# A gated cross-attention block on one core: exponent scores two steps behind the maximum scores, another owner of a bank's release, and GpSimd's rounding last in its step

## The reference, cut to what matters

```python
x = x + tanh(g_xattn[0]) * attention(layernorm(x), ctx, ctx)        # 16 heads, no projections, no mask
x = x + tanh(g_ffn[0])   * fp8_gemm(layernorm(x))                   # rounded to float8_e4m3, 256 x 256
x = x + tanh(g_xattn[1]) * masked_attention(layernorm(x), ctx)      # with projections q, k, v, o
x = x + tanh(g_ffn[1])   * ternary_ffn(layernorm(x))                # fake-quantised over the whole tensor
```

## Time and profile before

| | us |
|---|---|
| median of 3 runs | 3008.16 (3006.38 to 3012.38) |
| the profiled execution | 3008.19 |
| its span, first to last instruction | 3006.2 |

### The profile page before, as it was taken

How to read it: one execution, slowest core, us unless ns; L and a number is a source line. 1 busy time by engine, 2 the same in 40 slices (tenths; PEclk the granted TensorE clock), 3 DMA queues, 4 the chain that set the end, 5 groups by cost and what they waited for, 6 DMA issues and landing times. The chain is left out here.

```text
span 3006.2 us, 82393 instructions
## 1 busy us (share of the span) xinstructions
PE 2519.7 (84%) x28184; PEld 1800.6 (60%) x28184; DVE 2110.6 (70%) x6142; ACT 1789.5 (60%) x3015; POOL 1487.8 (49%) x2143
## 2 busy tenths in 40 slices
PE   3767777777777765999999999999999999999566
PEld 2445455555545544777777777777777777777344
DVE  4666666666666665778777877787778778878344
ACT  2666666666666663666566666665666666656355
POOL 2555555555555553444444544444444444444377
PEclk9998989899899997999999999999999999999756
DMA  2101111011110100000000000000000000000023
GB/s 68 33 29 31 31 31 31 28 31 31 31 31 28 32 14 17 18 19 18 19 19 16 21 17 18 19 18 19 19 19 18 16 19 19 18 19 13 22 101 102
DMA packets 99578, 82.87 MB, mean 28 GB/s; under 512 B 14928, under 2 KB 99280, under 8 KB 99280
## 3 DMA queue, kind: packets, MB, share of 16 engines
q1 hardware_dynamic: 99280, 78.88, 8.7%
HBM read 61.02 MB, written 16.78 MB: 26 GB/s over the span
## 5 line engine op out<-in xcount | busy, mean ns | idle before, releaser
L906 DVE TENSOR_REDUCE nmax<-bank_max 128x8 f32<-128x1024 f32 x256 | 312.6, 1221 | 371.5 <-DVEq L905 371.5
L617 ACT ACTIVATE stk<-bank_t 128x1024 bf16<-128x1024 bf16 x384 | 390.7, 1017 | 122.4 <-PE bank_t L1189 122.0
L649 ACT ACTIVATE stk<-bank_exp 128x1024 f32<-128x1024 f32 x256 | 262.0, 1023 | 201.7 <-ACTq L648 197.7
L622 ACT ACTIVATE probs<-bank_exp 128x512 f32<-128x512 f32 x512 | 288.8, 589 | 156.7 <-PE bank_exp L1169 156.7
L875 DVE TENSOR_REDUCE nmax<-bank_max 128x4 f32<-128x512 f32 x512 | 349.4, 683 | 31.9 <-PE bank_max L1156 31.7
L1218 PE MATMUL bank_max<-parts,QK 32*128 32x256 f32 x2048 | 333.2, 448 | 1.5 <-PEq L1281 1.5
L1225 PE MATMUL bank_exp<-parts,QK 32*128 32x256 f32 x2048 | 307.8, 421 | 0.0
L1189 PE MATMUL bank_t<-ident,parts 128*128 128x128 bf16 x4096 | 294.0, 220 | 2.6 <-PEq L1340 2.1
L487 POOL TENSOR_TENSOR rstd_f<-stat_f,eps_col 128x1 f32<-128x1 f32 x128 | 24.4, 191 | 522.5 <-POOLq L561 522.5
L1189 PEld LDWEIGHTS bank_t<-ident,parts 128*128 128x128 bf16 x4096 | 252.5, 98 | 21.6 <-issue 3.0
L1351 PE MATMUL bank_m<-wT,QK 128*128 128x256 f32 x1024 | 252.7, 391 | 1.2 <-PEq L1347 1.2
(11 more groups left out here) (181 smaller groups left out, 6647.5 us busy)
## 6 DMA issues: line engine op xcount, KB each, us to landing
X<-in_x SPq DMA_DIRECT2D x128, 128.0 KB, 2.1
stk<-in_ctx SPq DMA_DIRECT2D x128, 128.0 KB, 2.1
QK<-in_ctx SPq DMA_DIRECT2D x128, 128.0 KB, 2.1
out_y<-X SPq DMA_DIRECT2D x64, 256.0 KB, 2.1
ff_qq<-in_mask_BxSxS_ik SPq DMA_DIRECT2D x128, 64.0 KB, 1.9
stk<-shift_T SPq DMA_DIRECT2D x128, 8.0 KB
X<-in_L_xattn_Wq SPq DMA_DIRECT2D x1, 256.0 KB, 6.9
X<-in_L_xattn_Wk SPq DMA_DIRECT2D x1, 256.0 KB, 7.2
```

Source lines behind the costliest of these rows:

```text
L617: nc.scalar.activation(stk[k2][:, :, g * HG:(g + 1) * HG, :].rearrange("p w h t -> p w (h t)"), bank_tb[bank].rearrange("p (w n) -> p w n" ...
L622: nc.scalar.activation(probs[g % 2][:, :, :], bank_exp[g % 2][:, :, :], ACT.Exp, scale=SCALE).then_inc(probs_made, 1)
L649: nc.scalar.activation(a_probs[n], exp_pair[:, :, :, :].rearrange("p i h t -> p (i h) t"), ACT.Exp, scale=SCALE).then_inc(probs_made, 1)
L906: return v.tensor_reduce(nmax[:, n * H // 2:(n + 1) * H // 2], max_pair[:, :, :, :].rearrange("p i h t -> p (i h) t"), axis=AX.X, op=ALU.m ...
```

## The change

Six things change in pass A:

- Exponent scores are computed for batch i − 2 instead of i − 1; the shift transposes and their copy now have a step of their own in between. What follows them moves too: weighing at −2, the division at −3, the feed-forward part by 1 to 4 steps more.
- TensorE's step begins with `fill(0)`; then the transposes of weighed sums, the input transposes, the shift transposes, the feed-forward product (even steps), `fill(1)`, weighing 1, the transposes of rounded inputs (odd steps), weighing 0. Before `fill(0)` it waits for the second `max_read` of the previous step.
- VectorE signals `attn_read` itself when `attn_normed` has ended (before, GpSimd did when it took the residual); `attn_x` to GpSimd now comes with the following `bn_aggr`.
- GpSimd's step: statistics first (odd), masks, residual, V, and the rounding last (even steps); before, the rounding came first (odd) and the statistics last.
- ScalarE's step: exponential 1, copy of inputs, copy of shifts, copy of y (even), norms (feed-forward in odd steps, both attention inputs in even steps), exponential 0, copy of rounded inputs (odd), copy of weighed sums.
- Tiles: `sh_T`, `a_y` and the maxima (`a_nmax`) get two copies. New semaphores `stats_read`, `y_used`, `fq_used`. `hand_back` no longer drains. x is fetched one step earlier. 19 and 21 steps are unrolled at the ends instead of 12 and 15.

The diff, cut to its core:

```diff
-        sh_T = probs_b[1][:, 0:4 * P]
+        sh_T = [probs_b[1][:, n * 4 * P:(n + 1) * 4 * P] for n in range(2)]
...
-        A_LO, A_HI, A_FIRST, A_LAST = -6, NB + 5, 6, 6 + (NB - 12) // UNROLL * UNROLL
+        A_LO, A_HI, A_FIRST, A_LAST = -7, NB + 9, 12, 12 + (NB - 20) // UNROLL * UNROLL
...
             def hand_back():
-                mine(pool.drain())
+                if not own[0]:
+                    return
                 pool.wait_ge(pool_own, own[0])
...
+                if odd and (live(3) or live(-5)):
+                    s = k // 2 % 2
+                    pool.wait_ge(stats_made, 1)
...
+                    settle()
+                    pool.sem_inc(stats_read, 1)
...
+                if live(-3):
+                    pool.wait_ge(attn_x, 1)
+                    pool.sem_inc(attn_x, -1)
+                    nc.gpsimd.tensor_tensor(xs(i - 3), xs(i - 3), attn[:, :], ALU.add).then_inc(x_added, 1)
...
+                if not odd and live(-6):
+                    pool.wait_ge(grid_made, 1)
+                    pool.sem_inc(grid_made, -1)
+                    mine(nc.gpsimd.tensor_tensor(a_t, a_t, a_e, ALU.add))
                     settle()
+                    if live(-8):
+                        pool.wait_ge(fq_used, 1)
+                        pool.sem_inc(fq_used, -1)
+                    nc.gpsimd.tensor_tensor(ff_qq[:, :, :].rearrange("p b n -> p (b n)"), a_t, a_e, ALU.subtract)\
+                      .then_inc(fq_made, 1)
...
+                if live(-2):
+                    exp_pair_of(1)
                 if live(1):
                     act.wait_ge(in_Td, 1)
...
+                    nc.scalar.activation(sh_T[(k + 1) % 2], bank_tb[1][:, 0:4 * P], ACT.Copy).then_inc(shift_out, 1)
...
+                if not odd and live(2):
+                    for n in range(2):
+                        normed(a_xn[n], i + 2 + n, (k // 2 + 1) % 2, 2 + n).then_inc(xn_made, 1)
+                if live(-2):
+                    exp_pair_of(0)
...
+                if live(-3):
                     settle(n_rden)
-                    attn_normed().then_inc(attn_x, 1)
+                    attn_normed().then_inc(attn_read, 1)
+                if odd and (live(5) or live(-3)) and (live(1) or live(-7)):
+                    vec.wait_ge(stats_read, 1)
+                    vec.sem_inc(stats_read, -1)
...
+                if live(0):
+                    n_max = mine(max_pair_of(1, k % 2))
+                    settle(n_max)
+                    vec.sem_inc(max_read, 1)
+                    n_hi = mine(v.tensor_copy(sh_v[:, :, :, 0], a_nmax[:, k % 2, :].rearrange("p (i b) -> p i b", i=4)))
...
+                if not odd and live(-10):
+                    settle(n_y)
+                    v.scalar_tensor_tensor(xs2(i - 10), y.rearrange("p b n -> p (b n)"), gate[:, 2:3],
+                                           xs2(i - 10), ALU.mult, ALU.add).then_inc(y_used, 1)
...
-                now, last4 = k % RING, (k + 3) % RING
+                now = k % RING if live(0) else None
+                before = (k + 2) % RING if live(-2) else None
                 if live(0):
                     pe.wait_ge(m_made, 1)
                     pe.sem_inc(m_made, -1)
                 if live(-1):
-                    pe.wait_ge(shift_made, 1)
-                    pe.sem_inc(shift_made, -1)
...
+                    pe.wait_ge(max_read, 1)
+                    pe.sem_inc(max_read, -1)
+                fill(0, now, before, k % 2)
+                if live(-3):
+                    attn_transpose()
```

More of the change, by code:

```diff
@@ L243, in build @@
         norm_made = sem("norm_made")
+        stats_read = sem("stats_read")
+        y_used = sem("y_used")
+        fq_used = sem("fq_used")
         fx_made = sem("fx_made")
@@ L958, in step_a @@
                     settle()
                     vec.sem_inc(stats_made, 1)
-                if not odd and live(-4):
+                if odd and live(-5):
                     vec.wait_ge(fx_made, 1)
@@ L1206, in attn_transpose, with fill @@
                 last.then_inc(attn_back, 1)
[L1208 removed]
+            def fill(n, now, before, ring):
                 lo, hi = 2 * n, 2 * (1 - n)
@@ L1265, in step_a @@
                     last.then_inc(in_Td, 1)
+                if not odd and live(-8):
+                    pe.wait_ge(fq_out, 1)
+                    pe.sem_inc(fq_out, -1)
+                if live(-1):
+                    pe.wait_ge(shift_made, 1)
+                    pe.sem_inc(shift_made, -1)
+                    for b in range(4):
+                        last = nc.tensor.transpose(bank_tb[1][:, b * P:(b + 1) * P], sh[:, b * P:(b + 1) * P],
+                                                   ident[:, :])
+                    last.then_inc(shift_Td, 1)
+                if not odd and live(-8):
+                    for b in range(2):
+                        for c in range(DC):
+                            last = mm(bank_m[:, b * D:(b + 1) * D], ff_qT2[:, DC * b + c, :], f8_w[:, c, :],
+                                      start=c == 0, stop=c == DC - 1)
+                    last.then_inc(fy_made, 1)
+                if live(0):
+                    pe.wait_ge(max_read, 1)
+                    pe.sem_inc(max_read, -1)
+                if live(-2):
+                    pe.wait_ge(probs_made, 1)
+                fill(1, now, before, k % 2)
                 if live(-1):
```

183 lines of the change are left out of this document (73 added, 110 removed).

## The result

The changed kernel takes 2823.23 us (2821.82 to 2825.69, four runs) against 3008.68 us (3006.38 to 3012.38) for the kernel before on the same chip: a ratio of 0.938, with a 95% interval of 0.937 to 0.940. The forecast was 2808, with a range of 2745 to 2885. The profiled span went from 3006.2 to 2820.6 us.

The account below looks back on a forecast made before the run. No engine was full; a closed chain through four engines took turns for 8.0 us. 64 pairs going from 16.96 to 13.75 us save 205.4 us, the ends cost 5: 3008.2 − 200.4 = 2807.8 us, range 2745 to 2885.

Parts of the forecast that it names:

- the closed chain of the even step: Transposes, copy, scores, maximum, exponential and split of maxima in one even step: four engines take turns for 8.0 us.
- rival C: Changed pass: the clock still falls, pair 14.4 to 14.8 us, 2849 to 2873 us in all; chance 0.15.
- Rival D: Changed pass: clock stays at half, TensorE bounds at 19 us a pair, 3144 us; slower from 61% at half clock; chance 0.05.
- The walk: Following each engine's queue through a pair of steps from the even step's first scores; with collisions the pair is 13.75 us.
- The sum: Whole kernel: 64 pairs, each from 16.96 to 13.75 us, 205.4 us less, 5 more at the ends: 2807.8 us.
- its carrying term: VectorE's y addition and x update wait beside GpSimd's two roundings of 1.26 us; pair 13.75 us, without it 12.8.
- The signs named in advance: Profile marks of being right: pass about 200 us shorter, GpSimd roots 13.7 us apart, longer VectorE pieces, clock 0.97 or more.
- Bank release: VectorE frees the bank of weighed sums at the division's end: no gain, covered by the second scores.
- Drains: Two fewer per eight steps, on VectorE and GpSimd: between 0 and 2 us in all, taken as 0.
- Ends of the pass: Pipeline one to four steps deeper, nearly empty steps cost latencies: between 0 and 10 us, taken as 5.
- Other passes are untouched: Everything outside the changed pass: no change in time was counted.
- Rival B: Changed pass: roundings drift off VectorE's pieces, ScalarE's queue bounds; pair 12.8 to 13.2 us, 2747 to 2773 us; chance 0.16.

## Why the prediction was right, and where it was not

- **What bounded the kernel before.** That the closed chain of the even step is dear is borne out: putting its edge back into the changed kernels costs 288 to 390 us. Wrong was to set the pair of 15.92 us at full clock beside that of 17.99 at 0.81. The 15.92 are from the unrolled end of the pass, and the rows said so: VectorE has 21 instructions in that pair and 25 in the other. In the loop, a pair takes 16.7 to 16.8 us whether the clock is full or falls for 3.4 us, and one in four takes 18.06.
- **The price of the clock (rival C).** It was worked out from matmul times at both levels, with a pair of 19 us at half clock throughout; by that rate a fall of 3.4 us costs 0.9 us. Measured were 0 to 1.3 us in the kernel before, and 1.7 with the early low half. In the changed kernel it wasn't put to the test, since the clock didn't fall. (Rival D's 61% is a share of the pairs; by the rates that C uses it is 68% of the time.)
- **The walk.** Its times are good: second exponential of the even step at 4.87, measured 4.93 (508.77); second scores at 3.05, measured 2.87; next first scores 6.61, measured 6.66; odd maximum 9.15, measured 9.10; second scores 10.5, measured 10.43; second exponential 12.15, measured 12.31; next even scores 13.75, measured 14.18 (518.02).
- **Where 0.35 us a pair are missing.** The rounding started at 6.08 instead of 5.7. The y addition was to wait for the first rounding; it started first and ran free (0.43). So the update of x met the first rounding instead of the second, and the low half met the second. VectorE's chain ended at the same time, by another way (9.13 against 9.1). From there each small step was a little too short: statistics 9.35 instead of 9.3 and done at 11.19 instead of 11.05, norms 11.31 instead of 11.15, weighing 13.45 instead of 13.2.
- **The sum.** The 16.96 were a mean over the whole pass with its shorter pairs at the ends, the 13.75 a pair of the loop. From the first maximum to the last it was 1080.4 us (46.4 to 1126.7) and is 894.3 (44.2 to 938.5): 186.1 us less, where 205.4 were forecast. So the pairs gave 19 us too little, and the sum came out only 15 us too low because 2 us were gained ahead of the first maximum and 2.4 behind the pass, neither of which was in it.
- **Which collision carries the sum.** The prediction says that without collisions the pair would be 12.8. That step fails. With the update cut to four columns and the low half out of the rounding's way it is 13.69 undisturbed. The term that carried the sum is the order of GpSimd's queue (0.69 of 1.09 us); the collisions, which the prediction called its carrying term and which make up 0.95 us of it (13.75 against 12.8), are worth 0.40: 0.23 by the maximum that waits behind the low half, and 0.17 by the update, with up to 0.13 more that can't be told apart. The two causes were mixed because both start at the rounding, and the nearness of 13.75 to 14.10 doesn't tell them apart. And "the rounding last in an even step" is the same place in the queue as "first in an odd step" before: what the change moved was the statistics, from the end of the odd step to right behind the rounding, while GpSimd idles 3.6 us in the even step. The statistics in their old place, with the new lag, were not tried. The Trainium skill (SBUF — State Buffer, "Who interferes with whom") has it that the later of the two instructions fully blocks. The runs agree on the lock (4 columns, 0.90 us), but not for the whole instruction. An update of 0.75 ends 0.54 after GpSimd's operation, and one of 4 columns 0.02 after: so only a part of the update waits, and some 0.2 us of it do not.
- **The signs named in advance.** The update of x about 1.4 us long: 1.54. The second exponential of odd steps behind both norms: yes. Clock 0.97 or more: 1.00. Roots 13.7 apart: 14.10. The y addition over 1 us: no, 0.43. The low half at 1.30 was not named.
- **Bank release, priced at 0.** Right for the changed kernel. It was read from an even step alone; in the kernel before it is worth some 25 us of its own, by a wait in the odd step.
- **Drains, priced at 0 to 2 us.** Mis-sized: 13.6 us in the first pass (20 between the medians), once VectorE and GpSimd carry the pair. The bound came from the kernel before, in which they are hidden.
- **Ends of the pass, 5 us.** From the last maximum (1126.7 before, 938.5 after) to the second pass it took 27.9 us and takes 33.0: 5.1. The start of the pass, in which the first maximum comes 2.2 us earlier, was not looked at.
- **"Other passes are untouched".** 2.4 us came from behind the pass (1851.6 and 1849.2 us). The helper without its drain is used there too, but kernels with the same rest differ by up to 5.6 us there, so this is not shown to be its doing.
- **Rival B** (collisions hidden, 12.8 to 13.2) is no luck of drift but a matter of order: the rounding ahead of the masks gives it, 13.00. **Rivals C and D** didn't occur: the clock rose although TensorE still waits, for instance 1.37 us ahead of the even step's weighing.

## What to carry to other kernels

Taking a chain through four engines out by one more step of distance was worth more here than any other part of the change that was tried, and it also hides what is late elsewhere: the same edge cost 288 us with one order of GpSimd's queue and 390 with another. Before placing a long operation last in an engine's step, list what begins the next step on that engine and who waits for it; that cost 65 of the 250 us that were to be had here. Price small things, a drain or a signal from a busy queue, in the kernel in which their engine sets the time, and in both kinds of step: each of the two was nearly free in one kernel and 14 to 25 us in the other.

## What the runs showed of the hardware

- A VectorE operation with two SBUF inputs that starts beside a GpSimd operation ends shortly behind it: 0.54 to 0.55 us behind with 512 columns, which alone take 0.75, and 0.02 behind with 4 columns. That the part that waits is the streaming of the columns is my reading of these two. GpSimd pays as well: its rounding takes 1.27 us free and 1.47 beside the update.
- The granted clock was 1.00 from 200 to 900 us although TensorE stood idle for 1.37 us ahead of each even step's weighing and was busy for 76% of the pair. Before, with a hole of 1.26 us it was 0.90 in the same stretch; and once it was 0.98 there with the same pair. What decides between these the runs don't show. A fall of 3.4 us cost 1.7 us with the early low half (13.86 to 15.55), 1.3 in the kernel before without drains (16.78 to 18.05), and nothing in two places of the kernel before (16.77).
- A drain on VectorE and GpSimd cost about 0.4 us where they carry the pair (14.13 to 14.19 against 14.54 to 14.60), and nothing in the kernel before (16.77 with drains, 16.78 without).
